# A post-norm decoder layer on one core: the block sums of the feed-forward part move to GpSimd, and VectorE's and ScalarE's lists are reordered

## The chip, the core and the metric

The kernel runs on one core of a Trainium2 chip. The metric is the device time of one execution in microseconds (us); lower is better. A profiled execution also has a span, from its first to its last instruction, and every row below counts its times from the start of that span.

## What is computed

One decoder layer on x of shape 16 x 128 x 256 in fp32: a gated linear-attention block, a mixture of 8 experts, and a gated feed-forward network, each followed by a residual and a layer norm. Only the feed-forward part is touched:

```
def _tlin(x, w, s):
    return jnp.einsum('bsi,oi->bso', x, w) * s
...
h = jax.nn.silu(_tlin(x, w1_w, w1_s)) * _tlin(x, w2_w, w2_s)      # 256 -> 1024
h = jax.nn.gelu(_tlin(h, h1_w, h1_s), approximate=False)          # 1024 -> 1024
h = jax.nn.gelu(_tlin(h, h2_w, h2_s), approximate=False)          # 1024 -> 1024
return _tlin(h, w3_w, w3_s)                                       # 1024 -> 256
...
x = _layernorm(x + _L0_ffn_ref(x, ...), axis=-1)
```

The weights are ternary (-1, 0, 1) with a scale for each output.

## The kernel before

The five engines have one instruction list each, written out by hand and tied together by semaphores alone; each engine works through its list strictly in order. SyncE (SP) issues the transfers. An fp32 operand is split into a rounded high part (ScalarE, `high`, written to a ring of three tiles `hring`) and a low part (VectorE, `low_part`, operand minus high part, written in place as `part_r`), and TensorE multiplies a weight block by the high part (line 1513) and by the low part (line 1514).

The 2048 tokens are four groups of 512 rows (`N`), taken as two pairs, `ffn(0)` and `ffn(1)`; `q` is the pair. In a pair:

1. The first product: for each of two groups 8 units, each of 8 matmuls (line 1221). ScalarE applies silu (`gate_unit`), VectorE multiplies by the second branch (the operation in line 2103) and writes one of four blocks f11, f21 (first group), f12, f22 (second group). A block is 4 tiles of 128 x 512; `k` or `m` counts the tiles (`KH` = 4).
2. Two layers of 1024 x 1024 (`layer` 0 and 1), each as seven products of half-size blocks in place of eight (Strassen-Winograd), 32 matmuls each. Besides the four blocks, the products read t1 = f12 - f11, t2 = f22 - t1, t4 = f21 - t2, and t3 = f22 - f12, which overwrites f12. `first_sum`, `second_sum` and `fourth_sum` make t1, t2 and t4 on VectorE (lines 2017, 2024 and 2031); `third` makes t3 on GpSimd (line 807). The products read, in order, f11, f21, t2, t1, t3 (kept in f12), f22, t4 (`MOVING`). I call them products 0 to 6 of layer 0 and products 7 to 13, which are layer 1.
3. The last product (lines 1520 and 1521), with the rows of each group scaled, added and normed.

The results of a layer leave PSUM as snapshots (ScalarE, `snap`), additions (VectorE, `block_11`, `block_22`, `block_12`, lines 2037, 2043, 2049) and gelu (ScalarE, `curved`, line 1152). A product's first output tile needs all four low parts of its operand; the other three tiles find them there. TensorE also waits where a PSUM bank has not been read yet.

The work between the experts and the feed-forward part: the second group's rows are normed (`norm2_apply`), split into 16-bit halves (`norm2_halves`), turned by DMA (`turn_halves`), put together (`norm2_words`) and split again (`x_high`, `x_low`). All engines branch on `wide`, a flag that says whether the weights are ternary; here the first side is taken.

## Time and profile before

| | before |
|---|---|
| median of 3 runs | 773.61 us (773.35 to 773.98) |
| the profiled execution's own time | 772.94 us |
| its span | 771.0 us |
| mean granted TensorE clock | 0.993 of full speed |
| TensorE busy | 97% of the span |
| VectorE, ScalarE, GpSimd busy | 79%, 56%, 35% |

The busy shares cover the whole span; the change lies in its last 315 us. 1.9 us of the profiled time lie outside of its span.

### The profile page before, as it was taken

What the parts mean: (1) busy time and instruction counts of PE and PEld (TensorE: products, weight loads), DVE (VectorE), ACT (ScalarE), POOL (GpSimd) and SP (SyncE); (2) the same over time, 40 slices, a digit from 0 to 9 for tenths busy, and PEclk for the clock granted to TensorE, in tenths of its full rate; (3) what the DMA queues carried; (4) which work ended last, traced back from release to release, by engine and by line L of the source; (5) the groups of instructions that cost most, each with busy time, mean ns of one, the idle gap of its engine ahead of it and who ended that gap; (6) DMA issues with size and microseconds to landing.
All of it is one profiled execution on the core that took longest, in us unless ns stands there. A gap on an engine that the chain in (4) does not pass through costs nothing.

```text
span 771.0 us, 11852 instructions
## 1 busy us (share of the span) xinstructions
PE 750.3 (97%) x3699; PEld 632.6 (82%) x3699; DVE 605.3 (79%) x1294; ACT 430.2 (56%) x839; POOL 272.9 (35%) x293
## 2 busy tenths in 40 slices
PE   9999999999999999999999999899899998999995
PEld 7788988888888888888888887688787986887885
DVE  5789989876798989999676667967966569778566
ACT  6788743434555656555443346465677454646672
POOL 2777243225574747557252330301200203111003
PEclk9999999999999999999999999999999999999999
DMA  7800000004345445351731021144363101363201
GB/s 269 291 1 0 2 1 1 1 22 141 119 130 206 151 144 183 99 197 39 260 115 44 13 69 20 56 136 164 110 191 112 53 1 55 110 219 124 95 1 58
DMA packets 31706, 77.15 MB, mean 100 GB/s; under 512 B 8736, under 2 KB 13472, under 8 KB 27808
## 3 DMA queue, kind: packets, MB, share of 16 engines
q1 hardware_dynamic: 31360, 76.18, 29.4%
q8 instruction: 28, 0.46, 0.3%
q14 instruction: 30, 0.25, 0.1%
q10 hardware_dynamic: 288, 0.26, 0.1%
HBM read 58.08 MB, written 16.78 MB: 97 GB/s over the span
## 4 chain that ended last, share of the span: by engine, by line
PE 75%; DVE 14%; ACT 5%; issue 4%; POOL 1%; DVEq 0%; POOLq 0%; ACTq 0%
PE bank L1365 15%; PE bank L1249 8%; PE bank L1343 7%; PE bank L1344 7%; PE bank L1348 7%; PE bank L1513 6%; PE bank L1514 6%; PE bank L1364 6%; PE bank L1221 5%; DVE part_r L2012 3%; ACT hring L1135 3%; DVE part_f L2024 2%; DVE part_f L2031 2%; PE bank L1368 2%; DVE part_f L2103 2%
## 5 line engine op out<-in xcount | busy, mean ns | idle before, releaser
L1365 PE MATMUL bank<-wx_both,hx_hi 128*128 128x512 f32 x512 | 191.4, 397 | 0.0
L1513 PE MATMUL bank<-hring,wring 128*128 128x512 f32 x448 | 176.9, 395 | 8.0 <-DVE part_r L2012 5.9
L1514 PE MATMUL bank<-part_r,wring 128*128 128x512 f32 x448 | 175.8, 392 | 0.0
L992 ACT ACTIVATE hx_hi<-bank 128x512 fp32r<-128x512 f32 x128 | 76.5, 599 | 175.1 <-PE bank L1348 173.9
L710 POOL TENSOR_TENSOR x_tok<-right,x_tok 128x256 f32<-128x256 f32 x128 | 95.0, 743 | 173.3 <-ACT right L999 170.0
L2012 DVE TENSOR_TENSOR part_r<-part_f,hring 128x512 fp32r<-128x512 f32 x144 | 95.4, 687 | 51.6 <-ACT hring L1135 51.4
L1785 DVE SCALAR_TENSOR_TENSOR hx_lo<-bank,hx_hi 128x512 fp32r<-128x512 f32 x128 | 87.9, 687 | 51.4 <-ACT hx_hi L992 49.9
L1365 PEld LDWEIGHTS bank<-wx_both,hx_hi 128*128 128x128 f32 x512 | 96.0, 188 | 16.7
L1364 PE MATMUL bank<-wx_both,hx_lo 128*128 128x256 f32 x384 | 108.7, 283 | 0.0
L1513 PEld LDWEIGHTS bank<-hring,wring 128*128 128x128 f32 x448 | 85.2, 190 | 28.5 <-DVE part_r L2012 7.9
L1514 PEld LDWEIGHTS bank<-part_r,wring 128*128 128x128 f32 x448 | 85.3, 190 | 17.6
L1343 PE MATMUL bank<-xT_hi,wx_both 128*128 128x512 f32 x252 | 98.5, 391 | 0.0
L1344 PE MATMUL bank<-xT_hi,wx_both 128*128 128x512 f32 x252 | 98.1, 389 | 0.0
L1135 ACT ACTIVATE hring<-part_f 128x512 fp32r<-128x512 f32 x144 | 88.7, 627 | 12.3 <-DVE part_f L2024 7.1
L1348 PE MATMUL bank<-xT_lo,wx_both 128*128 128x512 f32 x252 | 77.6, 389 | 0.0
L1364 PEld LDWEIGHTS bank<-wx_both,hx_lo 128*128 128x128 f32 x384 | 72.8, 190 | 5.5 <-DVE hx_lo L1785 0.3
L1152 ACT ACTIVATE part_f<-part_f,scales 128x512 f32<-128x512 f32 x48 | 34.4, 721 | 66.7 <-DVE part_f L2037 34.3
L807 POOL TENSOR_TENSOR part_f<-part_f 128x512 f32<-128x512 f32 x16 | 27.7, 1734 | 119.6 <-DVE part_f L2103 61.6
L1794 DVE SCALAR_TENSOR_TENSOR x_tok<-bank,gates,x_tok 128x256 f32<-128x256 f32 (+1 forms) x128 | 61.2, 478 | 7.7 <-PE bank L1365 1.5
L999 ACT ACTIVATE right<-bank,gates 128x256 f32<-128x256 f32 x128 | 60.2, 470 | 9.3 <-DVE x_tok L1794 9.3
L1344 PEld LDWEIGHTS bank<-xT_hi,wx_both 128*128 128x128 f32 x252 | 47.3, 188 | 10.5
L1348 PEld LDWEIGHTS bank<-xT_lo,wx_both 128*128 128x128 f32 x252 | 47.3, 188 | 9.9
(204 smaller groups left out, 1431.7 us busy)
## 6 DMA issues: line engine op xcount, KB each, us to landing
wring<-h_dram SPq DMA_DIRECT2D x28, 1024.0 KB, 4.8
wx_raw<-in_wx SPq DMA_DIRECT2D x16, 512.0 KB, 7.9
raw_quads<-in_wffn SPq DMA_DIRECT2D x16, 512.0 KB, 5.7
h_dram<-sums SPq DMA_DIRECT2D x8, 1024.0 KB, 4.4
h_dram<-raw_quads SPq DMA_DIRECT2D x8, 512.0 KB, 6.5
stage<-in_wffn SPq DMA_DIRECT2D x12, 256.0 KB, 2.6
x_tok<-in_x SPq DMA_DIRECT2D x1, 2048.0 KB, 11.0
h_dram<-raw_quads SPq DMA_DIRECT2D x8, 256.0 KB, 6.7
```

The source lines that it names most:

```text
L710: pool.tensor_tensor(row, right[:, j % 2], row, ALU.add).then_inc(s_row_ok, 1)
L992: act.activation(hx_hi[:, place, c], bank[b][:, :], ACT.Relu).then_inc(s_relu_ok, 1)
L1135: act.activation(hring[n % 3][:, k], part[at_[name]][:, k], ACT.Copy).then_inc(s_h_hi, 1)
L1343: pe.matmul(bank[b][:, :], wi_hi[:, i, a], xT_hi[:, i, cols], start=(i == 0), stop=False)
L1344: pe.matmul(bank[b][:, :], wi_lo[:, i, a], xT_hi[:, i, cols], start=False, stop=False)
L1348: mm = pe.matmul(bank[b][:, :], wi_hi[:, i, a], xT_lo[:, i, cols], start=False, stop=(i == DC - 1))
L1364: pe.matmul(DBANK[j][:, 0:D], hx_lo[:, place, c, a], wo_h[:, c], start=False, stop=False)
L1365: mm = pe.matmul(DBANK[j][:, :].rearrange("p (h d) -> p h d", h=2), hx_hi[:, place, c, a], wo_hl[:, :, c], start=(c == 0), stop=(c == XC - 1))
L1513: pe.matmul(into[:, :], w, b_hi[:, k], start=(k == 0 and i in (0, 1, 3)), stop=False, skip_group_check=True)
L1514: mm = pe.matmul(into[:, :], w, b_lo[:, k], start=False, stop=(k == KH - 1), skip_group_check=True)
L1785: dve.scalar_tensor_tensor(out=hx_lo[:, place, c], in0=bank[b][:, :], scalar=0.0, in1=hx_hi[:, place, c].bitcast(F32), op0=ALU.max, op1=AL ...
L2012: dve.tensor_tensor(part_r[b][:, k], part[b][:, k], hring[n % 3][:, k].bitcast(F32), ALU.subtract).then_inc(s_h_lo, 1)
```

## The change

- GpSimd makes t1, t4 and t3 of each layer (`sums_of`: four t1, then four t4, then four t3); VectorE keeps t2 (`second_sum`). Since t1 reads f11 and t4 reads f21, and `low_part` overwrites both in place, `low_part` of f11 and of f21 now waits for GpSimd's sum. That makes 48 block sums on GpSimd, where 16 were, and 32 fewer on VectorE.
- VectorE's list: in the second group's units the low parts lag one unit behind; at the end of layer 0 three `block_12` stand together, then a low part of f11, the fourth `block_12`, and t2 alternating with low parts; `x_low` goes behind the low parts of f21.
- ScalarE's list: at the end of layer 0 the four high parts of f11 stand ahead of the gelu of f12, and `x_high` goes behind the gelu of f21.
- Product 5's output tiles wait for the snapshot of product 3 alone; product 6's wait for `block_22`.
- The second group's rows: norm, halves and the DMA's turning ahead of the branch; `norm2_words`, `x_high` and `x_low` one to two units earlier. GpSimd's root for these rows goes between the last expert's additions.

The core of the diff (left out: the counting of semaphores, the calls of `sums_of`, and the other side of the branch):

```diff
+            turn_halves(1)
+            sp_.wait_ge(s_wide_f, 1)
+            wide = sp_.value_load(wide_flag[0:1, 0:1], min_val=0, max_val=1)
+
...
-                    if u == 5 and last:
-                        ln_rstd(s_f_ve, s_f_rstd, 1)
+                    if u >= 5 and last and u < 7:
+                        ln_rstd(s_f_ve, s_f_rstd, u - 4)
             
             for p in range(1, E // 2):
                 pair(p, p == E // 2 - 1)
 
             pool.wait_ge(s_wide_f, 1)
             wide = pool.value_load(wide_flag[0:1, 0:1], min_val=0, max_val=1)
-
-            ln_rstd(s_f_ve, s_f_rstd, 2)
...
+            def first_sum(q, layer, k):
                 at_ = PARTS[layer]
+                pool.wait_ge(s_f_hf, (q * 2 + 1) * FC + k + 1 + 4) if layer == 0 else pool.wait_ge(s_h_act, q * 2 * 16 + 8 + k + 1)
+                pool.tensor_tensor(part[at_["t1"]][:, k], part[at_["f12"]][:, k], part[at_["f11"]][:, k], ALU.subtract).then_inc(s_h_pool, 1)
+
+            def fourth_sum(q, layer, k):
+                at_ = PARTS[layer]
+                pool.wait_ge(s_h_sum, second_done(q, layer, k))
+                if layer == 1:
+                    pool.wait_ge(s_h_act, q * 2 * 16 + 12 + k + 1)
+                pool.tensor_tensor(part[at_["t4"]][:, k], part[at_["f21"]][:, k], part[at_["t2"]][:, k], ALU.subtract).then_inc(s_h_pool, 1)
+
+            def third_sum(q, layer, k):
+                at_ = PARTS[layer]
+                pool.wait_ge(s_h_pool, pool_done(q, layer, "t1", k))
+                pool.tensor_tensor(part[at_["f12"]][:, k], part[at_["f22"]][:, k], part[at_["f12"]][:, k], ALU.subtract).then_inc(s_h_pool, 1)
+
+            def sums_of(q, layer):
                 for k in range(KH):
-                    pool.wait_ge(s_h_sum, summed(q, layer, "t1", k))
-                    if layer == 0:
-                        pool.wait_ge(s_f_hf, (q * 2 + 1) * FC + KH + k + 1 + 4)
-                    else:
-                        pool.wait_ge(s_h_act, q * 2 * 16 + 8 + k + 1)
-                    pool.tensor_tensor(part[at_["f12"]][:, k], part[at_["f22"]][:, k], part[at_["f12"]][:, k], ALU.subtract).then_inc(s_h_t3, 1)
+                    first_sum(q, layer, k)
+                for k in range(KH):
+                    fourth_sum(q, layer, k)
+                for k in range(KH):
+                    third_sum(q, layer, k)
...
-                    if q == 0 and m == 6:
+                    if q == 0 and m == 4:
                         x_high(1, xf_hi)
...
                         high(q, i0 + 6, m)
                         curved(q, layer, "f22", m)
+                    if layer == 0:
+                        for m in range(KH):
+                            high(q, i0 + 7, m)
                     for m in range(KH):
-                        if layer == 0:
-                            high(q, i0 + 7, m)
                         curved(q, layer, "f12", m)
                         if layer == 1:
                             high(q, i0 + 7, m)
-                    if q == 0:
-                        x_high(2 + layer, xf_hi)
                     for m in range(KH):
                         if layer == 1:
                             high(q, i0 + 8, m)
                         curved(q, layer, "f21", m)
                         if layer == 0:
                             high(q, i0 + 8, m)
+                    if q == 0:
+                        x_high(2 + layer, xf_hi)
...
                             elif i == 5:
+                                pe.wait_ge(s_h_snap, (q * 2 + layer) * 3 * KH + 8 + m + 1)
+                            else:
                                 pe.wait_ge(s_h_add, (q * 2 + layer) * 3 * KH + 4 + m + 1)
...
+                dve.wait_ge(s_f_T, J)
+                dve.wait_ge(s_f_keep, J)
+                norm2_apply(J, 1)
+                norm2_halves(1)
+
                 dve.wait_ge(s_gated_ok, B * E + 4)
                 dve.wait_ge(s_row_ok, B * E + 4)
                 dve.wait_ge(s_wide_f, 1)
                 wide = dve.value_load(wide_flag[0:1, 0:1], min_val=0, max_val=1)
                 dve.wait_ge(s_small_in, 32)
...
                     dve.wait_ge(s_h_hi, n * KH + k + 1)
+                    if layer < 2 and name in ("f11", "f21"):
+                        dve.wait_ge(s_h_pool, pool_done(q, layer, "t1" if name == "f11" else "t4", k))
                     dve.tensor_tensor(part_r[b][:, k], part[b][:, k], hring[n % 3][:, k].bitcast(F32), ALU.subtract).then_inc(s_h_lo, 1)
...
                                                  op0=ALU.mult, op1=ALU.mult).then_inc(s_f_hf, 1)
-                        if n == 4:
+                        if n == 3:
                             norm2_words(1)
-                        if n == 6:
+                        if n == 5:
                             x_low(1)
-                        if not first and m < KH:
-                            first_sum(q, 0, m)
-                            low_part(q, 0, m)
-                        elif not first:
+                        if not first and 1 <= m <= KH:
+                            low_part(q, 0, m - 1)
+                        if not first and m >= KH:
                             second_sum(q, 0, m - KH)
-                            fourth_sum(q, 0, m - KH)
-                            low_part(q, 1, m - KH)
+                        if not first and m > KH:
+                            low_part(q, 1, m - KH - 1)
+                    low_part(q, 1, KH - 1)
                     for layer in range(2):
...
-                        def behind(m):
-                            if layer == 0:
-                                first_sum(q, 1, m)
-                                low_part(q, i0 + 7, m)
+                        if layer == 0:
+                            for m in range(KH - 1):
+                                block_12(q, 0, m)
+                            low_part(q, i0 + 7, 0)
+                            block_12(q, 0, KH - 1)
+                            for m in range(KH):
                                 second_sum(q, 1, m)
-                            else:
-                                low_part(q, i0 + 7, m)
+                                if m < KH - 1:
+                                    low_part(q, i0 + 7, m + 1)
+                        else:
+                            block_12(q, 1, 0)
+                            for m in range(1, KH):
+                                block_12(q, 1, m)
+                                low_part(q, i0 + 7, m - 1)
+                            low_part(q, i0 + 7, KH - 1)
                         for m in range(KH):
-                            block_12(q, layer, m)
-                            if m > 0:
-                                behind(m - 1)
-                        behind(KH - 1)
+                            low_part(q, i0 + 8, m)
                         if q == 0:
                             x_low(g)
-                        for m in range(KH):
-                            if layer == 0:
-                                fourth_sum(q, 1, m)
-                            low_part(q, i0 + 8, m)
                     for i in (2, 3):
```

VectorE at the end of layer 0, before. `part0` is f12 of layer 1 in the making, `part7` its f11, `part5` its t1, `part2` its t2, `part6` the last operand of layer 0:

```order
L2012 TENSOR_TENSOR part6_r_146<-part6_f_147,hring0_130 128x512
L2043 TENSOR_TENSOR part1_f_137<-bank3,part1_f_137 128x512
L2049 TENSOR_TENSOR part0_f_135<-bank4,part0_f_135 128x512
L2049 TENSOR_TENSOR part0_f_135<-bank5,part0_f_135 128x512
L2017 TENSOR_TENSOR part5_f_145<-part0_f_135,part7_f_149 128x512
L2012 TENSOR_TENSOR part7_r_148<-part7_f_149,hring1_131 128x512
L2024 TENSOR_TENSOR part2_f_139<-part1_f_137,part5_f_145 128x512
L2049 TENSOR_TENSOR part0_f_135<-bank6,part0_f_135 128x512
L2017 TENSOR_TENSOR part5_f_145<-part0_f_135,part7_f_149 128x512
L2012 TENSOR_TENSOR part7_r_148<-part7_f_149,hring1_131 128x512
L2024 TENSOR_TENSOR part2_f_139<-part1_f_137,part5_f_145 128x512
L2049 TENSOR_TENSOR part0_f_135<-bank7,part0_f_135 128x512
```

The same place in the changed kernel (line numbers are its own; 2035 is `low_part`, 2042 `second_sum`, 2054 `block_22`, 2060 `block_12`):

```order
L2035 TENSOR_TENSOR part6_r_146<-part6_f_147,hring0_130 128x512
L2054 TENSOR_TENSOR part1_f_137<-bank3,part1_f_137 128x512
L2060 TENSOR_TENSOR part0_f_135<-bank4,part0_f_135 128x512
L2060 TENSOR_TENSOR part0_f_135<-bank5,part0_f_135 128x512
L2060 TENSOR_TENSOR part0_f_135<-bank6,part0_f_135 128x512
L2035 TENSOR_TENSOR part7_r_148<-part7_f_149,hring1_131 128x512
L2060 TENSOR_TENSOR part0_f_135<-bank7,part0_f_135 128x512
L2042 TENSOR_TENSOR part2_f_139<-part1_f_137,part5_f_145 128x512
L2035 TENSOR_TENSOR part7_r_148<-part7_f_149,hring1_131 128x512
```

The t1 rows (line 2017) are gone from this list, the first low part of f11 stands ahead of the fourth `block_12`, and each low part of f11 stands ahead of the next t2.

VectorE in the second group's units 4 and 5, before (`part3` is f22, `part5` is t2, `part6` is t4, `part1` is f21):

```order
L2103 SCALAR_TENSOR_TENSOR part3_f_141<-bank1,scales_54,silu_152 128x512
L2024 TENSOR_TENSOR part5_f_145<-part3_f_141,part4_f_143 128x512
L2031 TENSOR_TENSOR part6_f_147<-part1_f_137,part5_f_145 128x512
L2012 TENSOR_TENSOR part1_r_136<-part1_f_137,hring1_131 128x512
L2103 SCALAR_TENSOR_TENSOR part3_f_141<-bank3,scales_54,silu_152 128x512
```

Units 6 and 7 and what follows them in the changed kernel:

```order
L2114 SCALAR_TENSOR_TENSOR part3_f_141<-bank5,scales_54,silu_152 128x512
L2042 TENSOR_TENSOR part5_f_145<-part3_f_141,part4_f_143 128x512
L2035 TENSOR_TENSOR part1_r_136<-part1_f_137,hring1_131 128x512
L2114 SCALAR_TENSOR_TENSOR part3_f_141<-bank7,scales_54,silu_152 128x512
L2042 TENSOR_TENSOR part5_f_145<-part3_f_141,part4_f_143 128x512
L2035 TENSOR_TENSOR part1_r_136<-part1_f_137,hring1_131 128x512 x2
L2035 TENSOR_TENSOR part5_r_144<-part5_f_145,hring2_132 128x512 x4
```

A unit has lost its t4 row, and the low parts of t2 follow at once on the last two low parts of f21, where GpSimd's t4 and t3 rows now are due as well.

## Rows read from the trace of the kernel before

**Rows 1.** The page's first part: busy time of TensorE.

```profile
PE 750.3 (97%) x3699; PEld 632.6 (82%) x3699; DVE 605.3 (79%) x1294; ACT 430.2 (56%) x839; POOL 272.9 (35%) x293
```

**Rows 2.** Waits from 450 us on: engine, line, releaser, us in total, times, longest.

```profile
PE bank L1513 <- DVE part_r L2012: 5.9, 4, 2.6
PE bank L1221 <- DVE xf_lo L2055: 1.9, 1, 1.9
PE bank L1513 <- issue: 1.6, 1, 1.6
PE bank L1513 <- DVE part_f L2043: 0.5, 1, 0.5
```

**Rows 3.** Timeline of TensorE, pair 1: start us, us, engine, line.

```profile
640.57 0.39 PE L1513 MATMUL bank<-hring,wring 128*128 128x512 f32 x1
...
648.96 0.39 PE L1514 MATMUL bank<-part_r,wring 128*128 128x512 f32 x1
651.92 0.79 PE L1513 MATMUL bank<-hring,wring 128*128 128x512 f32 x1 [2.58 <-DVE part_r L2012]
...
697.53 0.50 PE L1513 MATMUL bank<-hring,wring 128*128 128x512 f32 x1 [0.43 <-DVE part_r L2012]
...
703.55 0.39 PE L1513 MATMUL bank<-hring,wring 128*128 128x512 f32 x1
```

**Rows 4.** Windows: length, busy time (instructions) by engine, granted clock, DMA share, GB/s.

```profile
472.20:475.40 3.20, 3.20 (x14) 2.66 (x15) 1.08 (x2) 1.55 (x3) 0.00 (x0) 1.00 0.00 0
498.20:501.40 3.20, 3.20 (x8) 2.54 (x9) 3.20 (x7) 0.64 (x1) 0.00 (x0) 0.51 0.06 26
651.90:655.10 3.20, 3.17 (x8) 2.56 (x9) 3.20 (x7) 0.73 (x1) 0.00 (x0) 0.53 0.06 23
```

**Rows 5.** Timeline of VectorE, pair 1: start us, us, engine, line.

```profile
648.06 0.74 DVE L2103 SCALAR_TENSOR_TENSOR part_f<-bank,scales,silu 128x512 f32<-128x512 f32 x1
...
649.63 1.64 DVE L2031 TENSOR_TENSOR part_f<-part_f 128x512 f32<-128x512 f32 x1
651.19 3.09 DVE L2012 TENSOR_TENSOR part_r<-part_f,hring 128x512 fp32r<-128x512 f32 x5
...
656.03 0.69 DVE L2012 TENSOR_TENSOR part_r<-part_f,hring 128x512 fp32r<-128x512 f32 x1
...
683.66 0.68 DVE L2043 TENSOR_TENSOR part_f<-bank,part_f 128x512 f32<-128x512 f32 x1
...
687.48 1.79 DVE L2024 TENSOR_TENSOR part_f<-part_f 128x512 f32<-128x512 f32 x1
...
696.80 0.68 DVE L2012 TENSOR_TENSOR part_r<-part_f,hring 128x512 fp32r<-128x512 f32 x1
```

**Rows 6.** Timeline of GpSimd, early stage of the kernel.

```profile
43.64 1.29 POOL L682 TENSOR_TENSOR qk<-q_sb,k_sb 128x512 f32<-128x512 f32 x1 [1.39 <-ACT k_sb L914]
44.89 1.75 POOL L667 TENSOR_TENSOR vT_lo<-vp,vT_hi 128x512 f32 x1
```

**Rows 7.** Timeline of VectorE at the same time.

```profile
43.66 1.82 DVE L1595 SCALAR_TENSOR_TENSOR sp<-al,sp 128x512 f32<-128x512 f32 x1
```

**Rows 8.** Timeline of VectorE before the feed-forward part.

```profile
455.82 0.48 DVE L1794 SCALAR_TENSOR_TENSOR x_tok<-bank,gates,x_tok 128x256 f32<-128x256 f32 x1 [0.61 <-PE bank L1365]
458.88 0.42 DVE L1774 TENSOR_SCALAR xn<-x_tok,mv,rstd 128x256 f32<-128x256 f32 x1 [2.57 <-POOL rstd L705]
```

**Rows 9.** Timeline of ScalarE at the end of layer 0, pair 1.

```profile
684.38 0.72 ACT L1152 ACTIVATE part_f<-part_f,scales 128x512 f32<-128x512 f32 x1 [1.36 <-DVE part_f L2043]
685.01 0.62 ACT L1135 ACTIVATE hring<-part_f 128x512 fp32r<-128x512 f32 x1
685.53 0.71 ACT L1152 ACTIVATE part_f<-part_f,scales 128x512 f32<-128x512 f32 x1
```

**Rows 10.** Groups by line from 450 us on: count, busy us, mean ns, idle before.

```profile
L807 POOL TENSOR_TENSOR part_f<-part_f 128x512 f32<-128x512 f32 x16 | 27.7, 1734 | 119.6 <-DVE part_f L2103 61.6 <-DVE part_f L2017 58.0
L2012 DVE TENSOR_TENSOR part_r<-part_f,hring 128x512 fp32r<-128x512 f32 x144 | 95.4, 687 | 51.6 <-ACT hring L1135 51.4
```

More of the change, by code:

```diff
@@ L633, in _ @@
                 for g in range(G - 1):
-                    turn_halves(g + 1)
+                    if g > 0:
+                        turn_halves(g + 1)
                     for t in range(g * J, g * J + J):
@@ L816, in ffn @@
             def ffn(q):
-                third(q, 0)
+                sums_of(q, 0)
                 if q == 0:
@@ L822, in ffn @@
                     ln_rstd(s_e_ve, s_e_rstd, 2)
-                third(q, 1)
+                sums_of(q, 1)
                 if q == 0:
@@ L2011, in low_part @@
                     dve.wait_ge(s_h_hi, n * KH + k + 1)
+                    if layer < 2 and name in ("f11", "f21"):
+                        dve.wait_ge(s_h_pool, pool_done(q, layer, "t1" if name == "f11" else "t4", k))
                     dve.tensor_tensor(part_r[b][:, k], part[b][:, k], hring[n % 3][:, k].bitcast(F32), ALU.subtract).then_inc(s_h_lo, 1)
-                def first_sum(q, layer, k):
-                    at_ = PARTS[layer]
-                    dve.wait_ge(s_f_hf, (q * 2 + 1) * FC + k + 1 + 4) if layer == 0 else dve.wait_ge(s_h_act, q * 2 * 16 + 8 + k + 1)
-                    dve.tensor_tensor(part[at_["t1"]][:, k], part[at_["f12"]][:, k], part[at_["f11"]][:, k], ALU.subtract).then_inc(s_h_sum, 1)
                 def second_sum(q, layer, k):
                     at_ = PARTS[layer]
-                    dve.wait_ge(s_h_sum, summed(q, layer, "t1", k))
+                    dve.wait_ge(s_h_pool, pool_done(q, layer, "t1", k))
                     if layer == 0:
@@ L2024, in second_sum @@
                     dve.tensor_tensor(part[at_["t2"]][:, k], part[at_["f22"]][:, k], part[at_["t1"]][:, k], ALU.subtract).then_inc(s_h_sum, 1)
-                def fourth_sum(q, layer, k):
-                    at_ = PARTS[layer]
-                    dve.wait_ge(s_h_sum, summed(q, layer, "t2", k))
-                    if layer == 1:
-                        dve.wait_ge(s_h_act, q * 2 * 16 + 12 + k + 1)
-                    dve.tensor_tensor(part[at_["t4"]][:, k], part[at_["f21"]][:, k], part[at_["t2"]][:, k], ALU.subtract).then_inc(s_h_sum, 1)
                 def block_11(q, layer, m):
```

31 lines of the change are left out of this document (15 added, 16 removed).

## The prediction

> **What bounds the kernel.** The page's first part comes first: TensorE is busy 97% of the span [rows 1], so a change can give back only what TensorE loses to waits. The list of waits from 450 us on shows what lies in the feed-forward part [rows 2]: 5.9 us for a low part (line 2012), 1.9 us for the second group's `x_low`, 1.6 us put down to "issue" (at the start of product 7 in pair 0), 0.5 us for a `block_22`. That is 9.9 us. The timeline of TensorE and the windows show what such a wait costs besides. In pair 1 TensorE starts product 0 at 640.57, stops after 648.96 and goes on at 651.92 [rows 3]; in the 3.2 us behind that stop it issues 8 matmuls at a granted clock of 0.53, against 14 in 3.2 us at full clock [rows 4]. So it runs at 1.2 GHz there in place of 2.4, and 6 matmuls of 3.2/14 = 0.23 us are missing: 1.4 us. Pair 0 has the same stop at 495 us, with the same stretch behind it at 0.51. Behind the 1.9 us wait the clock stays at 1.00 [rows 4]. Each pair thus loses 2.6 + 0.4 + 1.4 = 4.3 us or so at product 1 (0.4 is the refilling of the array around the stop, 2.96 us from 648.96 to 651.92 less one matmul of 0.23 and the 2.58), and all of the feed-forward losses together are 9.9 + 2 x 1.8, about 14 with their refilling.
>
> The second thing to read is how far VectorE and ScalarE lag behind TensorE, for a TensorE that no longer stops runs into whoever is next. The timeline of VectorE in pair 1 gives three marks [rows 5]:
> - mark A, the first low part of t1 (product 3's operand), at 656.03: 15.5 us after product 0 started;
> - mark B, the last `block_22` of layer 0, at 683.66, 27.6 us after A. In between, VectorE and ScalarE hand tiles to and fro, and nothing of this stretch's order changes;
> - mark C, the end of the last low part of f11 of layer 1, 696.80 + 0.60 = 697.40, 13.7 us after B. TensorE waits for it and goes on at 697.53 [rows 3].
>
> With no stop, seven products of 32 x 0.227 = 7.26 us (0.227 is 648.96 - 640.57 over the 37 matmuls between [rows 3]) bring TensorE to product 7 at 640.57 + 50.8 = 691.4, and it would want the fourth low part 1.4 us later, at 692.8. C lies at 697.4. So this chain, and not TensorE, sets the time of product 8 (703.55 [rows 3]), and the stop at product 1 is for the most part time that would be waited out at product 7. The question is what the change does to A and to C.
>
> **What a sum costs on GpSimd.** A block sum takes 1.29 us on GpSimd when it has SBUF to itself [rows 6]; the low part on VectorE has a mean of 0.69 us, with a new one every 0.60 [rows 5, 10]. The 16 sums that GpSimd makes now have a mean of 1.73 [rows 10], because the two engines hold each other up. VectorE's operation of two SBUF inputs that begins 0.02 us after GpSimd's takes 1.82 in place of 0.69: it is held up for 1.13 us, and GpSimd's next, queued directly behind, then takes 1.75, since VectorE had come first [rows 6, 7]. A second sum caught by t3 takes 1.79, held up for 1.11 [rows 5]. So where both have such work queued they take turns, 1.7 us a turn, in place of 0.6 for VectorE alone.
>
> The Trainium skill, SBUF — State Buffer, "Who interferes with whom", states this as a rule: a VectorE instruction with two SBUF inputs contends with a GpSimd instruction that reads SBUF, and the second to issue is blocked until the first is done. The rows agree, with 1.11 to 1.13 us of a sum's 1.29. By the rule's whole instruction a turn would cost 0.17 us more, which with ten turns in a pair would add some 3 us to the sum.
>
> **The change, step by step (in pair 1, then pair 0).**
>
> 1. Mark A. Today a unit of the second group costs VectorE the product, t2, t4 (held up, 1.64) and a low part; the last unit begins at 648.06 and the last low part of f21 ends at 651.8 [rows 5]. The changed list has neither t1 nor t4, so VectorE follows TensorE (a unit each 1.81 us) and has the last product done some 3.2 us after product 0 starts, at about 643.8. The fourth t2 and the third low part of f21 take it to 645.4 with one hold-up. The last low part of f21 now waits for GpSimd's fourth t4 (1.3 to 1.8 us), and then GpSimd's four t3 stand directly behind: this low part and three of t2's take turns with them, 4 x 1.7 us, so the first ends at about 649.0 and the third of t2 at 654.1. One more low part (0.6) and the rows' statistics, which take 1.8 us between the run of five low parts and A today [rows 5], put A at 656.5. That is 0.4 later than today, although TensorE is 4.3 us ahead. If t3 held up nothing, 4 x 1.1 us would be saved, and A would be 4 us earlier: the bound on this side. On the other side I allow another 1 us. TensorE itself finds product 1's last low part (649.0) just when it wants it (647.8 + 1.4 = 649.2), so the stop at product 1 is gone.
> 2. Mark C. From B: 0.7 until ScalarE sees `block_22`; a gelu, 0.63; now four high parts of f11 at 0.52 before the first gelu of f12, 0.7 [rows 9], so GpSimd starts t1 4.3 us after B, and ends at 5.6. Its second t1 is ready and takes SBUF at once; the first low part of f11 is held up and ends at 7.3. The fourth `block_12` stands behind it in VectorE's list (the second order piece), though its product was long done, and ends at 7.9; its gelu, 0.7, and the fourth t1, 1.3, follow at 10.1. In turns from there: the second low part ends at 10.7, second t2 against the first t4 12.4, third low part 13.0, third t2 against the second t4 14.7, fourth low part 15.3. C comes 15.3 us after B, in place of 13.7: 1.6 later. Bounds: 12.0, if the last three hold-ups don't happen; 16.5, if the handing over between GpSimd and the others takes 0.1 to 0.2 longer at each of eight steps.
> 3. The clock. Today TensorE waits 0.4 us at product 7 in pair 1. Now it arrives some 4 us ahead and gets the four low parts at 1.7 to 2.3 us each, with two matmuls (0.45 us) between. It is idle for over 4 us out of 6, more than the 2.6 us in a row that brought the clock to 0.53, though in pieces of 1 to 2 us like those that didn't. I take the fall, 1.4 us as behind today's stop; the bounds are 0 and 1.6.
> 4. Product 8 follows C as today, 703.55 - 697.40 = 6.1 us. So pair 1 is 0.4 + 1.6 + 1.4 = 3.4 us later. The 4.3 us of the stop at product 1 and the 0.4 at product 7 need no entry of their own: they lie ahead of C.
> 5. Pair 0 is the same, 3.4 us, less what it loses today outside of that chain. The second group's rows: `norm2_apply` starts at 458.88, while VectorE's last work before it starts at 455.82 and takes 0.48 [rows 8], so the rows come 2.5 us earlier, and the 1.9 us wait with its refilling, 2.1 us, is gone. Then, behind product 8, 0.3 of the waits for low parts (5.9 less 2 x 2.58 and 0.43 [rows 2, 3]) and the 0.5 for `block_22`, which product 5 no longer waits for, 1.3 us with their refilling. The 1.6 us at product 7 lie ahead of C too and give nothing. Pair 0: 3.4 - 2.1 - 1.3 = 0.
> 6. At nothing: GpSimd's root between the experts' additions (GpSimd is idle there, and the row additions' buffer of two gives it 1 us); the new wait for product 6, since `block_22` is done before it; `x_high` and `x_low` moved back, with a product of slack until they are read.
>
> Sum: +3.4 us. The profiled execution's span is 771.0 and its own time 772.94, 0.67 below the median of the runs shown; against the median, 773.6 + 3.4 = 777.0.
>
> **Rivals.**
> - *The clock holds at product 7* (12%). The waits there come in pieces, and behind pieces of 1.6 and 1.9 us the clock stayed up. Then both steps of 1.4 us fall away: 777.0 - 2.8 = 774.2, no measurable change.
> - *GpSimd holds VectorE up much less* (16%; the other side). Its mechanism is at A and C: t3 finds VectorE between two operations, and low parts slip in. It decides from about 1.7 us a pair, a fifth of the hold-ups counted in steps 1 and 2. If A came 4 us earlier and C 3 us, TensorE would be bound by itself, all but about 2 of the 14 us lost today would be gone: 762. Half of that way, which is likelier, is 768. Against it stands that today every t3 caught in such company holds VectorE up by 1.1 us.
> - *The chain through GpSimd is longer still* (10%). A 1 us later and C 1 us later in both pairs: 777.0 + 4 = 781. For it speaks that product 3 would then wait as well.
> - *The change doesn't do what it says*: the stop at product 1 stays, since the last low part of f21 waits for t4. By step 1 it is 0.2 us from being late; a slip there costs no more than it saves at product 7, so this has no time of its own.
>
> **Numbers.** The forecast case has 62%, with a range of its own of 775.3 to 778.8. The steps' bounds and the rivals give 771.0 to 780.0 for 8 in 10. About 0.2% (1.5 us) is what a measurement of this kernel can tell from no change: faster 0.16, same 0.12, slower 0.72.
>
> **What would show it.** Right: no wait at product 1 and for `x_low`; t3 and low parts alternating at 1.7 us behind the second group; a wait of TensorE at product 3 of up to 1.5 us; product 7 with three or four waits of 1 to 2 us and a clock near 0.5 behind it; GpSimd's sums with a mean near 1.5 us. Wrong: four low parts of f11 in a row at 0.6 us, or product 8 earlier than 62 us after product 0 (today 703.55 - 640.57 = 63.0). The prediction fails first if the hold-up of VectorE by queued GpSimd sums is not what the rows show of single ones.

## The result and the profile after

The changed kernel takes 776.38 us (median of 7 runs, 775.73 to 778.18), the kernel before 773.38 on the same chip: a ratio of 1.0035, 95% interval 1.0024 to 1.0046. By the ratio it is 2.7 us slower, by the two medians 3.0. The profiled execution's span is 774.4 us, 3.4 more than before.

TensorE's waits from 450 us on, which were [rows 2] before:

```profile
PE bank L1534 <- DVE part_r L2035: 9.1, 8, 1.6
PE bank L1534 <- ACT part_f L1170: 1.9, 1, 1.9
```

Nothing is waited for at product 1, for `x_low` or for a `block_22`, yet there are 11.0 us of waits in place of 9.9. The timeline of TensorE in pair 1 shows where they went (to be read beside [rows 3]; 1534 and 1535 are the two matmul lines, 2035 is the low part):

```profile
641.21 0.39 PE L1534 MATMUL bank<-hring,wring 128*128 128x512 f32 x1
...
693.55 0.39 PE L1535 MATMUL bank<-part_r,wring 128*128 128x512 f32 x1
694.60 0.50 PE L1534 MATMUL bank<-hring,wring 128*128 128x512 f32 x1 [0.67 <-DVE part_r L2035]
694.94 0.40 PE L1535 MATMUL bank<-part_r,wring 128*128 128x512 f32 x1
696.90 0.50 PE L1534 MATMUL bank<-hring,wring 128*128 128x512 f32 x1 [1.56 <-DVE part_r L2035]
697.24 0.40 PE L1535 MATMUL bank<-part_r,wring 128*128 128x512 f32 x1
699.20 0.65 PE L1534 MATMUL bank<-hring,wring 128*128 128x512 f32 x1 [1.56 <-DVE part_r L2035]
...
706.84 0.39 PE L1534 MATMUL bank<-hring,wring 128*128 128x512 f32 x1
```

Product 7 gets its tiles one at a time, with two matmuls between, and product 8 starts at 706.84, 65.6 us after product 0 (63.0 before). The windows behind the last of these stops (us; then busy time and instructions of TensorE, its weight loads, VectorE, ScalarE, GpSimd; the granted clock; DMA), of pair 1 and pair 0, show the clock at 1.2 GHz, as behind the stop at product 1 before [rows 4]:

```profile
699.20:702.40 3.20, 3.20 (x8) 2.52 (x9) 3.20 (x3) 1.12 (x2) 2.57 (x2) 0.53 0.00 0
545.90:549.10 3.20, 3.20 (x9) 2.43 (x8) 3.20 (x3) 1.12 (x2) 2.57 (x3) 0.50 0.01 3
```

VectorE's timeline in pair 1 has the marks of [rows 5]: behind the second group, A, B, and the four low parts of f11 with C at 698.47 + 0.60 = 699.07.

```profile
645.87 0.68 DVE L2035 TENSOR_TENSOR part_r<-part_f,hring 128x512 fp32r<-128x512 f32 x1
647.80 7.39 DVE L2035 TENSOR_TENSOR part_r<-part_f,hring 128x512 fp32r<-128x512 f32 x5 [1.25 <-POOL part_f L810]
...
656.94 0.69 DVE L2035 TENSOR_TENSOR part_r<-part_f,hring 128x512 fp32r<-128x512 f32 x1
...
683.83 0.68 DVE L2054 TENSOR_TENSOR part_f<-bank,part_f 128x512 f32<-128x512 f32 x1
...
689.44 1.70 DVE L2035 TENSOR_TENSOR part_r<-part_f,hring 128x512 fp32r<-128x512 f32 x1 [3.14 <-POOL part_f L803]
691.06 0.68 DVE L2060 TENSOR_TENSOR part_f<-bank,part_f 128x512 f32<-128x512 f32 x1
691.66 1.18 DVE L2042 TENSOR_TENSOR part_f<-part_f 128x512 f32<-128x512 f32 x1
692.77 1.78 DVE L2035 TENSOR_TENSOR part_r<-part_f,hring 128x512 fp32r<-128x512 f32 x1
694.47 1.77 DVE L2042 TENSOR_TENSOR part_f<-part_f 128x512 f32<-128x512 f32 x1
696.16 0.68 DVE L2035 TENSOR_TENSOR part_r<-part_f,hring 128x512 fp32r<-128x512 f32 x1
696.77 1.77 DVE L2042 TENSOR_TENSOR part_f<-part_f 128x512 f32<-128x512 f32 x1
698.47 0.68 DVE L2035 TENSOR_TENSOR part_r<-part_f,hring 128x512 fp32r<-128x512 f32 x1
```

Five low parts take 7.39 us, where five that nobody holds up take 3.1. GpSimd's own timeline beside it, t4 (line 810), t3 (815) and t1 (803), is what they take turns with:

```profile
646.03 1.67 POOL L810 TENSOR_TENSOR part_f<-part_f 128x512 f32<-128x512 f32 x1 [0.63 <-DVE part_f L2042]
647.66 6.37 POOL L815 TENSOR_TENSOR part_f<-part_f 128x512 f32<-128x512 f32 x4
...
688.04 4.25 POOL L803 TENSOR_TENSOR part_f<-part_f 128x512 f32<-128x512 f32 x3 [17.41 <-ACT part_f L1170]
692.58 1.42 POOL L803 TENSOR_TENSOR part_f<-part_f 128x512 f32<-128x512 f32 x1 [0.28 <-ACT part_f L1170]
693.96 1.73 POOL L810 TENSOR_TENSOR part_f<-part_f 128x512 f32<-128x512 f32 x1
```

The whole story fits in the four lengths from product 0 to product 8. The table has them for every kernel here, in pair 0 and pair 1, each read from the timelines as above, and behind them the time from product 8 of pair 0 to the start of the pair's last matmul of the products:

```
kernel              0 to A       A to B       B to C       C to 8      0 to 8       8 to end, pair 0
before              15.5 15.5   29.1 27.6   13.7 13.7   6.2 6.2   64.4 63.0   44.7
changed             15.7 15.7   29.0 26.9   15.2 15.2   7.9 7.8   67.9 65.6   43.4
e1 rows early       15.5 15.5   29.1 27.9   13.7 13.7   6.2 6.2   64.4 63.2   44.7
e2 gelu first       15.7 15.7   29.0 26.9   13.1 13.2   7.6 6.2   65.5 61.9   43.7
e3 t3 held          12.3 12.3   29.4 27.2   15.2 15.2   9.0 6.2   65.8 60.9   43.3
e4 layer 1 back     15.7 15.7   29.1 26.9   13.7 13.7   8.7 6.2   67.2 62.5   43.3
e5 filled           15.7 15.7   29.1 26.9   15.2 15.2   6.2 6.2   66.1 64.0   45.1
e6 e2 and e3        12.2 12.2   29.4 27.2   13.2 13.2   6.2 6.2   61.0 58.8   45.2
e7 layer 0 back     15.5 15.5   29.1 27.9   15.2 15.2   9.0 7.8   68.7 66.3   43.3
e8 e4 and e3        12.3 12.3   29.4 27.2   13.7 13.8   8.7 6.2   64.1 59.4   43.3
e9 before, t3 held  12.4 12.4   29.4 27.2   10.4 10.4   7.1 8.0   59.3 58.0   43.8
e10 e9 and rows     12.4 12.4   29.4 27.2   10.4 10.4   7.1 8.0   59.3 58.0   43.3
e11 t3 of layer 0   12.2 12.4   29.4 27.2   13.7 13.7   6.2 6.2   61.5 59.5   44.7
```

### The profile page after: what moved, and what is told of

Read it like the earlier page. It is cut to its first block, busy times and chain, and to the rows that moved or that the text cites. A ratio compares the mean times of both kernels' runs of the same rounds, so it can differ in the third digit from the quotient of the medians.

```text
span 774.4 us, 11867 instructions
## 1 busy us (share of the span) xinstructions
PE 752.5 (97%) x3699; PEld 632.8 (82%) x3699; DVE 604.6 (78%) x1262; ACT 430.5 (56%) x839; POOL 320.3 (41%) x325
## 4 chain that ended last, share of the span: by engine, by line
PE 80%; DVE 8%; issue 4%; ACT 3%; POOL 2%; DMA 1%; SPq 0%; DVEq 0%; ACTq 0%; POOLq 0%
PE bank L1384 15%; PE bank L1268 8%; PE bank L1240 8%; PE bank L1534 8%; PE bank L1535 8%; PE bank L1362 7%; PE bank L1363 7%; PE bank L1367 7%; PE bank L1383 6%; DVE part_r L2035 4%; ACT hring L1153 2%; PE bank L1387 2%; DVE part_f L2042 2%; PE bank L1541 1%; PE bank L1542 1%
## 5 line engine op out<-in xcount | busy, mean ns | idle before, releaser
L2035 DVE TENSOR_TENSOR part_r<-part_f,hring 128x512 fp32r<-128x512 f32 x144 | 118.5, 850 | 58.4 <-ACT hring L1153 48.9
L803 POOL TENSOR_TENSOR part_f<-part_f 128x512 f32<-128x512 f32 x16 | 23.4, 1473 | 83.9 <-ACT part_f L1170 49.7
L1363 PEld LDWEIGHTS bank<-xT_hi,wx_both 128*128 128x128 f32 x252 | 47.3, 188 | 10.6
```

The source lines that it names most:

```text
L1363: pe.matmul(bank[b][:, :], wi_lo[:, i, a], xT_hi[:, i, cols], start=False, stop=False)
L2035: dve.tensor_tensor(part_r[b][:, k], part[b][:, k], hring[n % 3][:, k].bitcast(F32), ALU.subtract).then_inc(s_h_lo, 1)
```

## The experiments

The theory: product 8 follows the chain A, B, C, and GpSimd's sums lengthen that chain wherever they take turns with a low part or a sum of VectorE's; the fall of the clock at product 7 comes on top. The rivals: the order of the lists does it and the turns are hidden; or the clock does it all. Ratios are to the kernel before on the same chip, 95% intervals behind them. The kernel before took 772.3 to 775.7 us in those runs, with medians of 774.6 to 775.0; the expectations count from 773.4, so what answers to them is 773.4 times the ratio.

**e1, the rows alone.** The kernel before with the parts of the change's diff that bring the second group's rows forward, and nothing on sums, lists or TensorE's waits:

```
+            turn_halves(1)
+            sp_.wait_ge(s_wide_f, 1)
...
+                norm2_apply(J, 1)
+                norm2_halves(1)
+
                 dve.wait_ge(s_gated_ok, B * E + 4)
```

> The kernel before, with one part of the change alone: the second group's rows (norm2_apply, norm2_halves, the first four transposes, the root on GpSimd, norm2_words, x_low and x_high one to two units earlier) ahead of the branch. Theory (the stop of 1.9 us for x_low is time of TensorE's own, and what follows moves with it, for VectorE's units follow TensorE): no wait for x_low, product 0 of pair 0 starts 2.1 us earlier after the first unit, time 1.9 to 2.1 us less than before, 0.9973 to 0.9975 of it. Rival (the 2.1 us are waited out at product 7 of pair 0, since the chain there doesn't move): the wait for x_low is gone, but product 8 of pair 0 starts as late as today, time within 0.3 us of before.

Measured: 770.28 us, 0.9947 (0.9934 to 0.9960), 4.1 us less; in the profiled executions 2.3 less (768.7 against 771.0). The wait for `x_low` is gone. From TensorE's first feed-forward matmul to product 0 of pair 0 it takes 29.1 us in place of 31.2, and everything behind keeps its lengths (the table) to 0.3 us. So the 2.1 us are TensorE's own, as expected. The further 1.8 us of the median don't show in the profiled executions: most of the runs of before on this chip had a lower mean granted clock, 0.989, than the 0.995 of four of e1's five. Whether that comes of the missing stop isn't shown; it could, for in e11 below the clock fell behind just this stop, which cost 1.5 us.

**e2, the gelu ahead of the high part.**

```
-                    if layer == 0:
-                        for m in range(KH):
-                            high(q, i0 + 7, m)
                     for m in range(KH):
                         curved(q, layer, "f12", m)
+                        if layer == 0:
+                            high(q, i0 + 7, m)
```

> The changed kernel, with ScalarE's list at the end of layer 0 in the other order: each gelu of f12 ahead of a high part of f11, so that the first gelu no longer stands behind four high parts (2.1 us). Theory of the chain (product 8 follows the last low part of f11, mark C, and C follows from GpSimd's first t1): t1 starts 2.1 us earlier after mark B, C 2.1 us earlier in each pair, with a fall of the clock at product 7 as in the changed kernel; time about 4 us less than the changed kernel, 772.4, or 1 us under the kernel before. If the shorter stops also keep the clock up, another 1.6 us a pair: 769. Rival (the turns that GpSimd and VectorE take set the pace, so that an earlier first t1 is waited out behind them): C less than 0.5 us earlier, time as the changed kernel, 776.4. Rival (clock alone): the stops get shorter, but the time doesn't move, 776.4, as long as the granted clock behind product 7 stays near 0.5.

Measured: 770.71 us, 0.9959 (0.9945 to 0.9973), or 770.2 on the expectation's scale; against 1.0035 of the changed kernel 5.9 us less. C comes 13.1 to 13.2 us after B, 2.1 less in both pairs: four high parts of 0.52 us, to a tenth. In pair 1 the clock held (C to 8 is 6.2), in pair 0 it fell again. Both rivals of this expectation fall. The new order of ScalarE's list, with the clock that falls behind its longer stops, cost more than the whole change did. What is left of the change in e2, the 32 sums on GpSimd and VectorE's lists, leaves C 0.6 us earlier behind B than the kernel before (13.1 against 13.7), and e2 and e1, which both have the early rows, 0.9959 and 0.9947, have intervals that overlap: the moved sums themselves cost nothing that these runs can tell. So the first half of the rival named at the start, that the order of a list does it, is right for the change's own loss; its second half, that the turns are hidden, is what e3 and e9 test.

**e3, the third sums held.** GpSimd waits ahead of the first t3 of layer 0:

```
+                if layer == 0 and k == 0:
+                    pool.wait_ge(s_h_lo, (q * (TILES_A_PAIR // KH) + 2) * KH + 4)
```

> The changed kernel, with GpSimd's four third sums of layer 0 held until VectorE has made the four low parts of t2, by a wait for them ahead of the first; nothing reads the third sums before the operand of product 6. Theory of the chain: mark A (the first low part of t1, 15.7 us after product 0 in the changed kernel) comes 3.3 to 4.4 us earlier, since four low parts are no longer held up for 1.1 us each, and B and C with it as far as TensorE lets them; no wait at product 3; the stops at product 7 shorter by 3 to 4 us, and with them the fall of the clock may go. Time 5 to 7 us less than the changed kernel, about 770.3. Rival (the sums cost the same wherever they stand: they then hold up the low parts of t1 and the block sums): A earlier, B not; time 776. Rival (A was not what set C, the turns at the end of layer 0 are all of the loss): B earlier by less than 1 us, time 775 to 776.

(The first to read them is in fact product 4.) Measured: 769.58 us, 0.9943 (0.9930 to 0.9955), 7.1 us less than the changed kernel, the edge of the 5 to 7 expected, though in pair 0 the clock fell by 2.8 us' worth (C to 8 is 9.0). VectorE's timeline at the place of the 7.39 us:

```profile
645.40 3.10 DVE L2037 TENSOR_TENSOR part_r<-part_f,hring 128x512 fp32r<-128x512 f32 x5 [1.25 <-POOL part_f L810]
648.42 1.40 DVE L2081 BATCH_NORM_STATS2 bn<-x_tok 128x6 f32<-128x256 f32 x4
```

Five low parts in 3.10 us: (7.39 - 3.10)/4 = 1.07 us for each t3 (in the 7.39 us the last low part of f21 and the first three of t2's are held up, and the fourth isn't), and A comes 3.5 us sooner. GpSimd makes its four t3 beside the rows' statistics then, in 5.57 us, 1.39 each. Of the 3.5 us, 0.35 are given back between A and B, where one low part is held up. The sums don't cost the same wherever they stand.

**e4 and e7, half of the change undone.** In e4 layer 1's t1 and t4 go back to VectorE:

```
+                            def behind(m):
+                                first_by_ve(q, 1, m)
+                                low_part(q, i0 + 7, m)
+                                second_sum(q, 1, m)
```

> Half of the change undone: layer 1's t1 and t4 are made by VectorE again, in the order of the kernel before (and ScalarE's f12 gelu with its high parts in the old order), while layer 0's stay on GpSimd, with the new lists and the rows split early. Theory of the chain: from B to C 13.7 us, as in the kernel before, instead of 15.2, so 1.5 us less a pair, and the clock at product 7 stays up or falls: between 3 us (it falls) and 6.5 us (it holds in both pairs) less than the changed kernel, and I expect it to hold in at least one pair: 770 to 772. Rival (the sums of layer 0 are the whole of the loss, by mark A): the time stays at 776. Rival (the clock alone): as soon as TensorE stands ahead of the chain by 3 us, the clock falls, whatever makes it wait: 773.4.

Measured: 769.65 us, 0.9937 (0.9924 to 0.9950), or 768.5, 1.5 under the expectation. B to C is 13.7 in both pairs again. The clock held in pair 1; in pair 0 it fell, by 2.5 us. There the first matmul of product 7 waits 3.65 us, put down to "issue". It needs a bank that ScalarE's first gelu of f21 reads, and that gelu stands behind the last of f12; ScalarE's timeline has it from 539.93 for 0.67 us, and the matmul starts at 540.70:

```profile
539.93 0.67 ACT L1179 ACTIVATE part_f<-bank,scales 128x512 f32<-128x512 f32 x1
540.70 0.47 PE L1542 MATMUL bank<-hring,wring 128*128 128x512 f32 x1 [3.65 <-issue]
```

This profiled execution, 771.65 us, is the slowest of e4's five, 2.0 above their median; whether the clock fell in the others isn't known.

In e7 layer 0's go back instead, with the old list of the second group's units:

```
+                        if not first and m < KH:
+                            first_sum(q, 0, m)
+                            low_part(q, 0, m)
+                        elif not first:
                             second_sum(q, 0, m - KH)
+                            fourth_sum(q, 0, m - KH)
+                            low_part(q, 1, m - KH)
```

> The other half of the change undone: layer 0's t1 and t4 are made by VectorE again, in the order of the kernel before; layer 1's stay on GpSimd with the new lists, and the rows stay early. Theory of the chain: A 15.47 after product 0 (15.72 in the changed kernel), the stop of 2.6 us at product 1 and the low clock behind it are back and cost nothing, C 15.2 after B; the stops at product 7 are 4 us less, so that the clock there may hold. From 2.2 us under the changed kernel (the clock falls in one pair) to 4 (in none): 772.5 to 774, about the kernel before. Rival (the stop at product 1 was time of its own, which the change does win): 4.3 us a pair more than the changed kernel, 785.

Measured: 776.37 us, 1.0019 (1.0009 to 1.0030). A stands 15.5 us behind product 0 and C 15.2 behind B, where the theory has them. The stop at product 1 (2.6 us) and the low clock behind it are back, and C, counted from product 0, is 0.7 us later than in the changed kernel in pair 1 and 0.2 earlier in pair 0: the rival's 785 is out. But I expected 772.5 to 774, and 773.4 times the ratio is 774.9, 0.9 more. Two things that I hadn't counted can make it up: A to B takes 1.0 us more in pair 1 (27.9 against 26.9), and in the profiled execution, at 777.68 us 1.3 above e7's median, the clock fell in both pairs although the stops at product 7 were fewer. How often it did so in the other runs isn't shown. The windows, in pair 1 and pair 0:

```profile
700.90:704.10 3.20, 3.20 (x9) 2.48 (x9) 3.20 (x3) 1.11 (x2) 2.57 (x3) 0.53 0.10 41
545.60:548.80 3.20, 3.20 (x9) 2.52 (x8) 3.20 (x4) 1.12 (x2) 2.57 (x3) 0.50 0.01 3
548.80:550.40 1.60, 1.60 (x5) 1.21 (x5) 1.60 (x2) 0.79 (x2) 1.60 (x2) 0.50 0.00 0
```

In pair 0, where the last stop ends at 544.94, it is still at 0.50 in the window from 4 to 5 us behind it.

**e5, the stops filled.** The changed kernel with matmuls that nobody reads, in the time that product 7 waits:

```
+                                if layer == 1 and i == 0 and m == 0 and k > 0:
+                                    pe.wait_ge(s_h_add, q * 2 * 3 * KH + 8 + 1)
+                                    for _ in range((2, 6, 4)[k - 1]):
+                                        pe.matmul(B1[0][:, :], wring[n % 4][:, 0, 0:P], b_hi[:, 0], start=True, stop=True, skip_group_check=True)
```

> The changed kernel, with 2, 6 and 4 matmuls more in each pair, ahead of the second, third and fourth tile of product 7's operand: they write into B1[0], which is free there and is started anew by product 8, and lie in time that TensorE waits in today (0.7, 1.56 and 1.1 to 1.56 us, against 0.45, 1.36 and 0.91 us for them). Nothing else is changed, so marks A, B and C stand where they did. Theory (the stops themselves cost nothing, C sets product 8; only the fall of the clock behind them is a term of its own): the clock stays at 1.00 behind product 7, product 8 follows C by 6.15 us as in the kernel before instead of 7.8 to 7.9, 1.6 to 1.8 us less a pair, time 773 and equal to the kernel before. Rival (the fall isn't TensorE's idle time but comes whatever it does, or the added matmuls delay the real ones): product 8 follows C by 7.8 us or more, time 776.4 or more.

Measured: 774.37 us, 0.9997 (0.9988 to 1.0006): the kernel before, and by the ratios 2.9 us under the changed one. A, B and C don't move; the clock does. The windows behind product 7, pair 1 and pair 0, have 14 matmuls in place of 8 and 9:

```profile
698.95:702.15 3.20, 3.20 (x14) 2.67 (x15) 3.20 (x3) 1.72 (x4) 2.57 (x2) 1.00 0.00 0
545.12:548.32 3.20, 3.20 (x14) 2.67 (x15) 3.20 (x3) 2.00 (x5) 2.57 (x2) 1.00 0.01 3
```

Product 8 follows C by 6.16 us in both pairs. In pair 0 it starts early enough to run into the next wait, 1.35 us at the fourth product of layer 1, which is why its last length grows by 1.8. So in the profiled executions 3.4 are won and 1.8 given back, and the spans differ by 1.5 (772.9 against 774.4), about half of what the ratios say.

**e6 and e8, two edits at once.** e6 has the edits of e2 and e3, e8 those of e4 and e3.

> The changed kernel with the edits of e2 and e3 together: third sums of layer 0 held behind the low parts of t2, and each gelu of f12 ahead of a high part of f11. If the chain is a sum, as e2 and e3 say one at a time: A at 12.3 us after product 0, B 27.3 (pair 1) and 29.4 (pair 0) after A, C 13.15 after B, product 8 6.15 after C, or 59 and 61 us from product 0 to product 8 (65.6 and 67.9 in the changed kernel), with another 1.4 to 2.8 if the clock falls in pair 0. Time 11 to 13.5 us under the changed kernel, 763 to 765, about 0.988 of the kernel before. TensorE needs 58.1 us by itself for eight products, so hardly anything is left to gain at this place. Rival (one edit takes the other's gain, since TensorE or a new wait in the list binds as soon as one is done): the better of the two, 769.5.

> e4 (layer 1's t1 and t4 on VectorE, in the old order) with the third sums of layer 0 held as in e3. By the sum of the marks: A 12.3, B 27.3 and 29.4 after it, C 13.7 after B, product 8 6.15 after C: 59.5 and 61.6 us from product 0 to product 8, 1.4 to 2.8 more where the clock falls. Time 763.5 to 766, within 1.5 us of e6. Rival (as in e6, the gains don't add up): 769.5.

Measured: e6 764.49 us, 0.9874 (0.9859 to 0.9889); e8 763.73 us, 0.9863 (0.9848 to 0.9878). The lengths add up to a tenth (the table), and both beat the kernel before, by 9.7 and 10.6 us. On the expectations' scale they are 763.6 and 762.8, e6 within its 763 to 765 and e8 0.7 under its 763.5. The rival, that one edit takes the other's gain, falls. In e8 the clock fell in pair 0, in e6 in neither.

**e9, e10 and e11, the kernel before with t3 held.** If t3's turns are the loss, the kernel before has it too. e9 is that kernel with this alone (`(2, 2)[layer]` is 2 in both layers; e11 has `layer in (0,)` in the condition, so that it holds in layer 0 alone):

```
                 for k in range(KH):
+                    if k == 0 and layer in (0, 1):
+                        pool.wait_ge(s_h_lo, (q * (TILES_A_PAIR // KH) + layer * PRODUCTS + (2, 2)[layer]) * KH + 4)
                     pool.wait_ge(s_h_sum, summed(q, layer, "t1", k))
```

> The kernel before, with one edit alone: GpSimd's third sums, the only block sums that it makes there, are held in both layers until VectorE has made the four low parts of t2 (product 2's operand), by one wait ahead of the first; product 4 is the first to read them. VectorE keeps t1, t2 and t4. Theory of the chain (what lengthens it is GpSimd's sums taking turns with VectorE's, and the kernel before has that too): the t4 of the second group no longer take 1.64 us but 0.69, so A comes some 4 us earlier (11.5 us after product 0) and the stop at product 1 goes, with the low clock behind it; behind B the t2 of layer 1 take 0.69 in place of 1.78, so C comes 3.3 us earlier (10.4 us after B). Then TensorE binds by itself, but for the rows' 1.9 us and small stops: product 8 some 58.5 to 60 us after product 0, time 10 to 12 us under the kernel before, 0.985 to 0.987. Rival (the held sums come at a worse place: they hold up the low parts of t1 and f12's operand for product 4 is late): a wait at product 4, time within 2 us of before. Rival (e3's gain was the change's own and has nothing to give in the kernel before): same time.

> The kernel before, with the third sums held in layer 0 alone. Theory: A and with it B some 4 us earlier and no stop at product 1, but C still 13.7 us after B, so that product 7 waits again (1 us in pair 1, 2.6 us in pair 0); time 6 to 8 us under the kernel before, 0.990 to 0.992, between before and e9. Rival (A alone mattered, layer 1's turns are hidden): as e9. Rival (only layer 1's turns mattered): as before.

Measured: e9 762.05 us, 0.9853 (0.9833 to 0.9873), 11.4 us less; e11 767.83 us, 0.9915 (0.9900 to 0.9930), 6.6 less. The rivals of both fall. The groups of e9's sums (2026 is t2, 2033 t4, 809 GpSimd's t3; least, median and greatest ns of one, and from when to when) show the turns gone. In the kernel before the same view has medians of 1222, 1158 and 1724 ns for these three.

```profile
L2026 DVE TENSOR_TENSOR part_f<-part_f x16: 683/690/694, 484.0 to 684.8; 128x512 f32<-128x512 f32 x16
L2033 DVE TENSOR_TENSOR part_f<-part_f x16: 682/691/695, 484.7 to 689.0; 128x512 f32<-128x512 f32 x16
L809 POOL TENSOR_TENSOR part_f<-part_f x16: 1282/1296/1820, 496.9 to 697.3; 128x512 f32<-128x512 f32 x16
```

In pair 1 product 8 follows product 0 by 58.0 us, which is eight products of 7.26: TensorE has no stop at all there, and C is no longer what it waits for (so the 8.0 from C to product 8 has no fall of the clock in it). A came 3.1 us sooner, not the 4 of the expectation.

e10 adds the rows' early start and the new wait of product 5, which are parts of the change.

> e9 with the two parts of the change that stand apart from the sums: the second group's rows early (e1) and product 5 not waiting for block_22. If all is additive: another 2 to 2.5 us, with no wait at x_low nor for block_22; time 12 to 14 us under the kernel before, 0.982 to 0.984, and 1.5 to 3 us under e6 and e8. Rival (e9 already leaves TensorE waiting at product 7, where the earlier rows are waited out): as e9.

Measured: 760.12 us, 0.9817 (0.9803 to 0.9831), 14.2 us less than before, and the best here. Against e9 that is 2.8 us by the ratios and 1.9 by the medians (2 to 2.5 expected). It is 4.4 us under e6 and 3.6 under e8, more than the 1.5 to 3 expected; in the profiled executions most of this lies in pair 0, where e6 takes 61.0 and 45.2 us, e8 64.1 and 43.3, and e10 59.3 and 43.3. TensorE's row on its page, and all that it waits for from 450 us on:

```profile
PE 745.5 (98%) x3699; PEld 631.2 (83%) x3699; DVE 593.4 (78%) x1294; ACT 430.4 (57%) x839; POOL 268.0 (35%) x293
```

```profile
PE bank L1516 <- issue: 1.0, 1, 1.0
```

## Why the prediction was right, step by step

- **Mark A: right.** 15.7 us after product 0 in both pairs (15.9 by step 1), with the last low part of f21 and three of the four of t2 in turns with t3, and the stop at product 1 gone. TensorE waits 1.0 us at product 3, as the text allowed. e3 shows the cause by taking it away.
- **Between A and B: missed in pair 1, 0.7 us.** The prediction said that nothing changes there. It is 26.9 us in place of 27.6. In the kernels that stop at product 1 in pair 1 (before, e1, e7) it is 27.6 to 27.9, in those that don't and leave t3 where it was (changed, e2, e4, e5) 26.9. In the kernel before the first low part of product 6's operand waits 0.8 us for its high part in this stretch. That stands in ScalarE's list behind the snapshot of product 3's last tile (line 1141), and the snapshot waits for TensorE, which is through product 3 33.3 us after product 0, and 30.4 in the changed kernel. So the stop at product 1 was not hidden to the last tenth.

```profile
674.02 0.60 ACT L1141 ACTIVATE part_f<-bank 128x512 f32<-128x512 f32 x1 [0.56 <-PE bank L1514]
675.17 0.69 DVE L2012 TENSOR_TENSOR part_r<-part_f,hring 128x512 fp32r<-128x512 f32 x1 [0.80 <-ACT hring L1135]
```

- **Mark C: right.** 15.2 us after B in both pairs (15.3); the four low parts end at 7.2, 10.6, 12.9 and 15.2 (7.3, 10.7, 13.0, 15.3). e2 and e4 take it apart: the four high parts ahead of the first gelu are 2.1 us, undoing the sums and the orders together gives back 1.5, and so the moved sums with VectorE's list are worth 0.6 the other way. Two of the step's terms don't add up as written: 0.7 + 0.63 + 4 x 0.52 + 0.7 is 4.1 and not 4.3 (measured, 688.04 - 683.83 = 4.2), and 7.9 + 0.7 + 1.3 is 9.9 and not 10.1.
- **The clock: right in the profiled execution, 1.8 and 1.6 us (1.4),** and shown by e5 to be a term of its own. But its size is not fixed: over the kernels here in which product 8 waits for C, the time from C to it exceeds 6.2 us by anything from nothing to 2.8. And three of the changed kernel's seven runs had a mean granted clock of 0.985 and took 777.2 to 778.2 us, the others 0.991 and 775.7 to 776.4: that the one value of 1.4 came so near is in part luck. By the ratios e5 takes 2.9 us off, as much as the change's whole loss, in the profiled executions 1.5; the rival in which the clock holds (774.2) is what e5 made, 0.9997 of before.
- **Pair 0: right.** From the first feed-forward matmul to product 0 of pair 0 2.1 us less (2.1), behind product 8 1.3 less (1.3), and from the first feed-forward matmul to product 0 of pair 1 184.97 us against 184.95: nothing, as predicted.
- **The sum.** Pair 1: 0.3 + 1.5 + 1.6 - 0.7 = 2.7 (3.4); pair 0: 0. Most of the other 0.7 of the span's 3.4, 0.6, lies ahead of the feed-forward part, which starts at 456.24 in place of 455.62. I take that for scatter: e1, with the same early rows and roots, starts it at 455.18, and the kernels here range from there to 456.43. By the ratio the loss is 2.7, so the 0.7 too much in the forecast are the 0.7 between A and B that it had at nothing; the other terms miss by 0.2 at most each.
- **What was said of the stop at product 1.** The prediction has 0.4 us of refilling in it, but 2.96 - 0.23 - 2.58 is 0.15; its total of 4.3 us is about right all the same (product 2 starts 11.5 us after product 1, 4.2 more than a product's 7.26). It lies ahead of C and enters no sum.
- **The rival of the smaller hold-up** is out: 1.07 us each in e3. The Trainium skill, SBUF — State Buffer, "Who interferes with whom", lets the second to issue wait for the whole of the first instruction; the runs have 1.07 to 1.13 of a sum's 1.29 us. The same page of the Trainium skill, "Summary: rules for kernel authors", says of the two engines to schedule whichever is off the critical path: e9 does that with t3 alone, and the runs agree, with 11.4 us less.

What stays open: why the clock falls behind one group of stops and not behind another of the same lengths. It wasn't tried on a stretch by itself.

## What to carry to other kernels

Work on GpSimd isn't free because GpSimd is idle: where one of its sums met a VectorE operation with two SBUF inputs, it held it up by nearly its own length (1.07 to 1.13 of 1.29 us), so place it by what VectorE makes at that moment. Here one wait, which puts the 16 sums that GpSimd had behind VectorE's urgent ones, was worth 11 us, while giving it 32 more gained nothing that could be told. The change's own loss came of a list: four high parts stood ahead of the gelu on which the chain hung, and with the clock they cost 5.9 us. And value a stop of TensorE at the next point that the other engines' chain sets: those at product 1 looked like 4.3 us each, and were worth 0.7 to 1.0 in pair 1 and nothing in pair 0.

## What the runs showed of the hardware that I had not expected

- The clock falls behind stops that are short one by one: in the changed kernel behind 0.67, 1.56 and 1.56 us with two matmuls between each, and in pair 1 of e7 behind 0.2 and 1.56 us; in pair 1 of e3 and pair 0 of e6 it held behind 0.72 and 1.57, and 0.79 and 1.55 us. Behind the same 1.9 us stop for `x_low` it held in the kernel before and in e9 and fell in e11 (product 0 of pair 0 at 488.47 against 486.97 in e9, with the same program up to there).
- A fall at product 7 cost 1.4 to 2.8 us of lost matmuls. The scatter between executions goes with it in part: the kernel before took 772.3 us at a mean granted clock of 0.994 and 775.0 at 0.989 on one chip, and e5, filled, stayed within 773.8 and 775.0 at 0.994 to 0.997.
- Filling a stop with matmuls that write to a free bank kept the clock at 1.00 at no cost that the marks show.
